# A transformer kernel's last block: shorter fills between the row transfers, and a stage order written for that pace

## The reference, cut to what matters

```python
# per batch b, x[b] is 1024 x 128
x = x + ga * layernorm2(y + relu(y @ ff1_w.T + ff1_b) @ ff2_w.T + ff2_b)
h = layernorm(x) * (1 + cb) + sb
probs = softmax(h @ Wr)                       # 8 experts
p, e = top_k(probs, 2)                        # two experts for each token
pos = how many entries of this batch chose the same expert before
keep = pos < 160                              # capacity of an expert
buf[e, pos] = h                               # 8 x 160 rows
out = relu(buf @ W1[e] + b1[e]) @ W2[e] + b2[e]
x = x + gb * sum over the two choices of p * keep * out[e, pos]
```

## Time and profile before

| what | value |
|---|---|
| median of 3 runs | 1436.42 us (1435.21 to 1439.76) |
| the profiled execution's own time | 1436.2 us |
| its span, first to last instruction | 1434.5 us |
| mean granted clock of TensorE | 0.956 of full |
| tail: first TensorE work | 1153.8 us |
| tail: first send issued, last fill ended | 1226.5, 1370.8 us |
| busy over the whole span: TensorE, VectorE, ScalarE, GpSimd | 89%, 74%, 64%, 38% |

### The profile page before, as it was taken

One profiled execution on the slowest core, in us unless ns is written; L12 is line 12 of the kernel. 1 busy time (PEld: TensorE's weight loads), 2 busy tenths in 40 slices (PEclk: granted clock), 3 DMA queues, 4 the chain that ended last, 5 costly groups with the idle time before them and its releaser, 6 DMA issues. The chain is left out here.

```text
span 1434.5 us, 28628 instructions
## 1 busy us (share of the span) xinstructions
...
## 2 busy tenths in 40 slices
...
DMA packets 112673, 93.96 MB, mean 65 GB/s; under 512 B 20034, under 2 KB 98336, under 8 KB 112544
## 3 DMA queue, kind: packets, MB, share of 16 engines
...
...
## 5 line engine op out<-in xcount | busy, mean ns | idle before, releaser
L2446 ACT ACTIVATE probs<-scores_ps 128x1024 f32<-128x1024 f32 x512 | 507.0, 1027 | 88.3 <-PE scores_ps L2473 81.0
L2473 PE MATMUL scores_ps<-q_pack,k_pack 64*128 64x512 f32 x1024 | 245.9, 493 | 37.7 <-ACT probs L2446 23.1
L2490 PE MATMUL pv_ps<-probs,v_pad 128*32 128x512 f32 x2048 | 276.0, 612 | 0.1
L2473 PEld LDWEIGHTS scores_ps<-q_pack,k_pack 64*128 64x128 f32 x1024 | 96.4, 185 | 310.9 <-issue 152.4
L2366 POOL TENSOR_TENSOR squares<-sparse_scores 128x512 f32<-128x512 f32 x32 | 41.0, 1280 | 476.3 <-DVE sparse_scores L2611 476.2
L1406 ACT ACTIVATE hidden_experts<-pre_experts 128x512 f32<-128x512 f32 x94 | 59.3, 631 | 129.6 <-DVE pre_experts L1340 71.0
L2683 DVE TENSOR_SCALAR_CACHE_REDUCE junk<-sparse_scores,at 128x1024 f32<-128x1024 f32 x96 | 122.7, 1279 | 3.4
L1428 PE MATMUL up_ps_experts<-x_t_experts,up_weights_now_experts 128*128 128x128 f32 x752 | 107.1, 288 | 17.9 <-ACT hidden_experts L1406 8.1
L1428 PEld LDWEIGHTS up_ps_experts<-x_t_experts,up_weights_now_experts 128*128 128x128 f32 x752 | 94.8, 198 | 23.5 <-DVE up_weights_now_experts L1335 14.0
L1435 PE MATMUL down_ps_experts<-weights_t,hidden_experts 128*128 x736 | 98.5, 278 | 0.0
L3277 POOL DMA_INDIRECT expert_rows_dram<-expert_input_tail,send_to_tail x64 | 65.0, 1015 | 86.4 <-DVE expert_input_tail L3421 68.9
...
## 6 DMA issues: line engine op xcount, KB each, us to landing
q_pack<-q_pieces_dram SPq DMA_DIRECT2D x120, 64.0 KB
k_pack<-k_pieces_dram SPq DMA_DIRECT2D x120, 64.0 KB
...
```

What stands on the lines that cost most here:

```text
L2446: act.activation(probs[:, kt % 2, 2 * pair : 2 * pair + 2, c * 512 : c * 512 + 512], scores_ps[n % 2][:].rearrange("p (h t) -> p h t", h=2 ...
L2473: ins = pe.matmul(scores_ps[n % 2][:, head * 512 : head * 512 + 512], k_pack[group % 2][rows, pair, kt * P : kt * P + P].bitcast(F32R), q_ ...
L2490: ins = pe.matmul(pv_ps[32 * j : 32 * j + 32, c, :], v_pad[:, group % 2, kt, j, :], probs[:, kt % 2, j, c * 512 : c * 512 + 512], start=(k ...
```

## The change

Two edits, both in the tail. `SPACER` goes from 1024 to 512, so `unread` and each of the 64 fills have half the columns. And `TAIL_ORDER` is replaced: the same stages, each once, in another sequence. No stage's own code is changed. (The two lists are long. Shown are the stretch around batch 0's first send and the one around the last mixes of batch 0; the text of the prediction counts the work in the full lists.)

```diff
 TAIL_ORDER = """
...
-ff_relu.2.2 ff_up.2.3 ff_up.3.0 ff_relu.2.3 keep_n1.4 invert3.0 ff_up.3.1 root2.1
...
-best.0 ff_up.5.0 root2.3 ff_relu.4.3 keep_n1.6 ff_up.5.1 turn_n1.7 invert2.3 exps.0 pos.0 invert3.2 y_res.4 ff_down.4 index.0 norm3.2 gate.0 update.3
-send.0.0 turn_n3.2 ff_relu.5.0 keep_n3.2 send.0.1 ff_up.5.2 ff_out.4 ff_relu.5.1 logits.2 root3.3 ff_relu.5.2 ff_up.5.3 send.0.2 keep_y2.6 ff_up.6.0
...
-send.1.13 relu.0.6.1 turn_y.0.1 bias.0.5 go_up.0.7.0 keep_y.0.1 go_up.0.7.1 relu.0.7.0 go_down.0.6 send.1.14 relu.0.7.1 turn_y.0.2 bias.0.6 mix.0.1
-keep_y.0.2 send.1.15 turn_y.0.3 go_down.0.7 keep_y.0.3 send.2.0 load_x.1 mix.0.2 bias.0.7 send.2.1 turn_y.0.4 mix.0.3 keep_y.0.4 send.2.2 sg.1 gt.1.0
-turn_x.1.0 gt.1.1 turn_x.1.1 keep_x.1.0 send.2.3 gt.1.2 mix.0.4 gt.1.3 keep_x.1.1 gt.1.4 gt.1.5 send.2.4 turn_x.1.2 add.0.0 keep_x.1.2 gt.1.6 store.0
...
-gt.3.9 turn_y.3.3 bias.3.7 mix.3.1 keep_y.3.3 turn_y.3.4 mix.3.2 keep_y.3.4 mix.3.3 mix.3.4 add.3.0 add.3.1 store.6 store.7
...
+ff_up.3.2 ff_relu.3.1 attended.7 logits.0 root2.2 keep_n3.1 ff_up.3.3 ff_relu.3.2 logits.1 invert2.2 root1.7 ff_relu.3.3 ff_up.4.0 best.0 keep_y2.4
+y_res.3 ff_down.3 update.2 exps.0 ff_up.4.1 pos.0 ff_relu.4.0 gate.0 root3.2 ff_up.4.2 ff_relu.4.1 turn_n1.5 ff_relu.4.2 index.0 ff_up.4.3 keep_n1.5
+turn_n1.6 ff_relu.4.3 invert3.2 ff_up.5.0 send.0.0 keep_n1.6 ff_up.5.1 ff_out.3 norm3.2 y_res.4 ff_down.4 send.0.1 keep_y2.5 invert1.7 send.0.2
...
+go_up.0.7.1 relu.0.7.0 pos.3 gate.3 keep_x.1.0 turn_x.1.1 relu.0.7.1 send.2.5 turn_x.1.2 mix.0.1 keep_x.1.1 index.3 keep_x.1.2 send.2.6 bias.0.5
...
+go_down.1.3 gt.1.4 send.3.0 go_up.1.5.0 gt.1.5 go_up.1.5.1 relu.1.5.0 bias.1.3 mix.0.4 send.3.1 relu.1.5.1 send.3.2 go_down.1.4 gt.1.6 load_x.2
+add.0.0 go_up.1.6.0 send.3.3 go_up.1.6.1 bias.1.4 relu.1.6.0 add.0.1 turn_y.1.1 go_down.1.5 relu.1.6.1 gt.1.7 send.3.4 turn_y.1.2 go_up.1.7.0 bias.1.5
+keep_y.1.1 mix.1.0 relu.1.7.0 store.0 send.3.5 sg.2 send.3.6 turn_x.2.0 keep_y.1.2 store.1 go_up.1.7.1 go_down.1.6 keep_x.2.0 send.3.7 relu.1.7.1
...
+relu.3.7.1 bias.3.5 keep_y.3.2 go_down.3.6 mix.3.1 gt.3.8 bias.3.6 gt.3.9 go_down.3.7 turn_y.3.3 bias.3.7 mix.3.2 keep_y.3.3 turn_y.3.4 mix.3.3
+keep_y.3.4 mix.3.4 add.3.0 add.3.1 store.6 store.7
 """
...
-SPACER = 1024
+SPACER = 512
```

More of the change, by code:

```diff
@@ L3017 @@
[L3017 to L3020, removed]
@@ L3025 @@
[L3025 to L3028, removed]
@@ L3029 @@
[L3029 to L3032, removed]
@@ L3041 @@
[L3041 to L3044, removed]
@@ L3045 @@
[L3045 to L3056, removed]
@@ L3057 @@
[L3057 removed]
+turn_ctx.0 cols keep_ctx.0 dense.0 colk turn_ctx.1 attended.0 turn_ctx.2 keep_ctx.1 keep_ctx.2 dense.1 turn_ctx.3 root1.0 turn_ctx.4 invert1.0
+keep_ctx.3 dense.2 attended.1 turn_ctx.5 norm1.0 keep_ctx.4 dense.3 root1.1 turn_n1.0 invert1.1 keep_ctx.5 keep_n1.0 turn_ctx.6 attended.2 norm1.1
+ff_up.0.0 ff_up.0.1 dense.4 ff_relu.0.0 root1.2 ff_up.0.2 ff_relu.0.1 invert1.2 keep_y2.0 turn_n1.1 ff_up.0.3 attended.3 ff_relu.0.2 keep_n1.1
@@ new lines @@
+update.5 send.0.13 gate.1 root3.5 send.0.14 pos.1 ff_relu.7.0 ff_up.7.1 invert3.5 send.0.15 ff_up.7.2 ff_relu.7.1 index.1 norm3.5 ff_up.7.3 ff_out.6
+load_x.0 send.1.0 logits.4 ff_relu.7.2 turn_n3.5 ff_relu.7.3 send.1.1 root2.6 y_res.7 ff_down.7 keep_n3.5 invert2.6 send.1.2 update.6 send.1.3 sg.0
+root3.6 turn_x.0.0 invert3.6 turn_x.0.1 keep_x.0.0 send.1.4 logits.5 ff_out.7 norm3.6 turn_x.0.2 send.1.5 keep_x.0.1 best.2 root2.7 turn_n3.6
+keep_x.0.2 send.1.6 keep_n3.6 go_up.0.0.0 go_up.0.0.1 relu.0.0.0 send.1.7 relu.0.0.1 go_up.0.1.0 gt.0.0 pos.2 exps.2 invert2.7 send.1.8 go_down.0.0
@@ new lines @@
+index.2 go_up.0.1.1 relu.0.1.0 send.1.9 gate.2 relu.0.1.1 logits.6 go_up.0.2.0 go_up.0.2.1 send.1.10 update.7 relu.0.2.0 relu.0.2.1 go_up.0.3.0
+send.1.11 go_up.0.3.1 bias.0.0 root3.7 gt.0.1 go_down.0.1 send.1.12 invert3.7 relu.0.3.0 bias.0.1 norm3.7 gt.0.2 go_down.0.2 send.1.13 gt.0.3
+go_up.0.4.0 bias.0.2 turn_y.0.0 relu.0.3.1 turn_n3.7 gt.0.4 send.1.14 keep_n3.7 go_up.0.4.1 keep_y.0.0 go_down.0.3 relu.0.4.0 send.1.15 relu.0.4.1
+go_up.0.5.0 logits.7 relu.0.5.0 bias.0.3 gt.0.5 go_up.0.5.1 send.2.0 load_x.1 go_down.0.4 best.3 relu.0.5.1 turn_y.0.1 go_up.0.6.0 send.2.1
```

37 lines of the change are left out of this document (26 added, 11 removed).

## The result

The kernel before took 1435.82 us in the median of four runs (1433.95 to 1439.76), the changed one 1412.83 (1412.28 to 1414.63): a ratio of 0.9842, with a 95% interval of 0.9823 to 0.9862. That is 23.0 us less, where 14.9 were forecast. The profiled execution took 1412.28 us, with a span of 1410.6.

A forecast was written before the change was run, and what follows sets the result against it. GpSimd's sends and fills bound the last block's start, then mostly TensorE. Sends win 26 + 4.5 us, half reaching the end: last mix at 1416.2 against 1431.1, a gain of 14.9, so 1421.5 us, range 1412 to 1433.

The forecast's parts named there:

- part 1, the fill: GpSimd in the last block: a 512-column fill takes 0.55 us, a send 1.84 instead of 2.255, 26 us less in all.
- Part 2, the earlier start: Less TensorE and VectorE work before pos.0: GpSimd's first send starts 4.5 us earlier, at 1222.0, bounds 3 to 6.
- the 2 us to spare: Batch 1's rows addressed at about 1249, GpSimd free for them at 1251.4, so its sends would not wait.
- a sign that it is wrong: Batch 1's addresses so late that GpSimd waits; the other such sign was a send cycle above 2.0 us.
- Part 3, the arrivals: Sent rows loaded for TensorE: batch 0's at 1256.9 instead of 1267.3, batch 1's at 1286.3.
- The cover of two us: Batch 2's load waits for mix.0.4, 6.9 us of TensorE work ahead of turn_x.2.0, against 4.96 us of load.
- rival C: Slower: loads of batches 2 and 3 lie bare, TensorE leaves them at half clock; 1444 us, chance 0.08.
- Part 4, the hold on VectorE: VectorE's casts and place tiles during sends are held to the fill's end: 0.40 instead of 0.55 us an operation, factor 0.73.
- Rival A: VectorE, 97% full during the sends, is the new pace: a gain of 5 to 9 us, some 1429.5, chance 0.20.
- The losses after turn_x.1.0: TensorE's time beyond its counted work in the last three segments: 6, 3 and 5 us.
- Rival B: TensorE takes nearly all of it back, no gain: 1434 to 1438 us, chance 0.09.
- Rival D: Everything runs as listed, 8 instead of 15 us lost after turn_x.1.0: 1414 us, chance 0.13.

The follow-up runs named there:

- pace_only: The kernel before with only the fill shortened from 1024 to 512 columns, old order kept: 1422.41 us, ratio 0.9901 to the kernel before.
- order_only: The kernel after with fills set back to 1024 columns, new order kept: 1432.35 us, ratio 0.9961 to the kernel before.
- fill_256: The kernel after with fills of 256 instead of 512 columns: 1384.83 us on another chip, ratio 0.9783 to the kernel before.
- late_sends: The kernel after with six extra waited-for fills ahead of batch 0's first send: 1392.03 us on its chip, ratio 0.9831 to the kernel before.
- bias_first: The kernel after with VectorE's bias.1.2 moved ahead of keep_y.1.0: 1411.72 us, ratio 0.9822 to the kernel before.
- late_fills: The kernel after with 40 more waited-for fills on GpSimd behind the last send: 1411.22 us, ratio 0.9816 to the kernel before.
- after_again: The kernel after, unedited, measured once more: 1410.24 us, ratio 0.9821 to the kernel before.
- old_bias: The kernel before with VectorE's bias.3.6 moved ahead of keep_y.3.2: 1432.4 us, ratio 0.9976 to the kernel before.
- fill_8: The kernel after with fills of 8 instead of 512 columns: 1384.75 us on another chip, ratio 0.9786 to the kernel before.

## Why the prediction was right, and where its numbers were off

The mechanism held: shorter fills and an earlier first send bring the rows sooner, and TensorE's own work takes part of that back. The size is partly luck. 23.0 us were won for 14.9, and the measured interval (0.9823 to 0.9862, or 1410.4 to 1416.0 us) reaches below the range's end of 1412; the second measurement of the same kernel, 0.9821, comes to 1410.1 on the first one's scale.

**What bounds the block, and part 1, the fill: right.** 0.57 us in the mean for 0.55, 1.85 us a send for 1.84, the last fill ended at 1338.1 for 1339.5. pace_only alone brought 14 us; the whole change brought 23.

**Part 2, the earlier start: mis-sized.** Within the block the first send came 7.5 us earlier (65.2 for 72.7 us after the entry) where 4.5 were taken, with 6 as the upper bound. Of that, 5.4 us are pos.0 (62.7 for 68.1 after the entry; the count of TensorE's work had given 4.8). The other 2.1 are behind pos.0: the send follows it by 2.5 us instead of 4.6, because gate.0 stands ahead of index.0 now, with no invert between. The prediction counted only what stood ahead of pos.0. That the list alone does this is shown by order_only (64.9). The addresses of batch 1 came when forecast (index.1 ended at 1248.65, for about 1249), but GpSimd was free for them at 1248.2 instead of 1251.4: 2.4 us from the first send, the rest from the first 15 sends, which took 1.81 us each. So the 2 us to spare were gone and GpSimd waited 1.0 us for the addresses. The prediction had named just this as a sign that it is wrong. The sign came true and meant little: the wait put batch 1's rows off by 1.0 us, and without it the 64 sends kept to the forecast 1.84 us. The expectations of fill_256 and late_sends, which put this wait down to norm3.3, had the wrong row.

**Part 3, the arrivals: right for batch 1, some 3.7 us early.** At turn_x.0.0 TensorE's work was to end at 1254.7 and the load to come at 1256.9; TensorE was there at 1254.89 and the rows before it, so it didn't wait. turn_x.1.0 at 1283.55 for 1287.3: 2.4 from the first send, 0.5 from a landing and load of 6.8 instead of 7.3, and the 1 us of slips that did not come; the sends, with their wait of 1.0 us, gave back 0.2. The load did end TensorE's wait, as forecast. Its 4.39 us were a short one: it took 5.66 to 5.86 in the profiles of bias_first, late_fills and after_again. The load of batch 2 was issued at 1319.80, when mix.0.4 was done; the longest of this profile's four loads took 4.7 us, so it was there by 1324.5, and turn_x.2.0 ran at 1326.54. The cover of two us held (2.0 or more), and rival C had no part in it.

**Part 4, the hold on VectorE: right in direction, mis-sized.** Forecast was a factor of 0.73, from 0.55 to 0.40 us an operation. Measured: 0.16 a place tile (648 less 487) and 0.16 a cast (454 less 294), for 0.67 and 0.36 before. The step that failed is "such an operation is held to the end of the fill: up to 0.6 + 0.965. With the short fill 0.6 + 0.55". With fills of 1024 columns that holds, by the recorded spans. In the profiles of the kernel before and of order_only all 55 casts and place tiles that took over 0.06 us more than alone ended 0.15 us (casts) or 0.28 us (place tiles) after the end of a fill. With 512 columns it mostly doesn't: of the 20 such operations in the kernel after, 13 ended 0.09 us (casts) or 0.22 us (place tiles) after the fill had begun. This is one of the casts, and GpSimd's rows at the same time:

```profile
1301.23 0.86 DVE L3459 CAST gated_out_pieces_tail<-gated_out_tail 128x256 bf16<-128x256 f32 x1
```

```profile
1301.03 0.98 POOL L3278 DMA_INDIRECT expert_rows_dram<-expert_input_tail,send_to_tail  x1 [0.28 <-POOL unread_tail L3281]
1302.01 0.55 POOL L3281 MEMSET unread_tail<- 128x512 f32 x1
```

It started 0.2 us into the send and ended at 1302.10; to the end of the fill it would have been 1302.56. The cast at 1328.06 of the kernel before waited the whole fill out. Rival A, VectorE as the new pace, falls with the size: during the sends VectorE was busy for 88.2 us of 118.5, 74%, where 112 of 116 had been counted. The smaller hold, 0.16 for 0.40 us on 55 operations, is some 13 of the 24 us between; the rest stays open.

**The losses after turn_x.1.0: mis-sized, 14 forecast, 8.7 measured.** By window 43.0 for 35.1, 33.8 for 33.5 and 46.8 for 46.3, so 7.9, 0.3 and 0.5, where 6, 3 and 5 had been carried over from the old list. The step that failed is this carrying over: a loss of before is a property of its list. The loss at the end is in the kernel before (7.4) and in pace_only (5.6), and not in order_only (0.5), and 3.4 us of the 7.4 are one bias behind one keep_y, as old_bias shows. The forecast saw that bias gone and still kept 5. The first of the three windows took more than forecast: the wait of go_down.1.3 with its half clock is the new list's own, of the same make. Taking it away (bias_first) removed it from the trace but moved no time that could be measured; why the timed runs don't gain from it stays open.

**The sum.** 9.1 us separate the end of the last mix (1407.1) from its forecast (1416.2): 3.7 from the arrivals and 5.3 from the losses. "From turn_x.1.0 on TensorE is the bound" held in the last two windows, where it is busy throughout; in the one before them it is busy for 37.75 us of 43.00. Rival B, no gain, falls with the first measurement. Rival D had the number right (8 us lost), and it had no mechanism of its own; the one that the runs show is the order at the end of the list.

The Trainium skill (SBUF — State Buffer, Who interferes with whom) has a VectorE operation in a two-port mode block GpSimd for its whole length if it was issued first. What the prediction drew from this, that shorter fills would put more sends in the way of place tiles and so lengthen the sends, is not to be seen: the sends averaged 991 ns for 1015 before, and 998 in fill_8.
